# One decoder layer on one core: small weights first, the input projection in two transfers, sums and last roundings of the feed-forward weights on ScalarE

## What is computed

```python
def weight_quant(w):
    wf = w.astype(jnp.float32)
    s = 1.0 / jnp.clip(jnp.mean(jnp.abs(wf)), EPS, None)
    return (jnp.clip(jnp.round(wf * s), -1.0, 1.0) / s).astype(w.dtype)
...
x = x + _L0_attn_ref(_layernorm(x, axis=-1), L0_attn_W_in, L0_attn_conv_w, L0_attn_conv_b, L0_attn_dt_bias, L0_attn_A_log, L0_attn_D_param, L0_attn_norm_w, L0_attn_W_out)
x = x + _L0_xattn_ref(_layernorm(x, axis=-1), ctx_2048, mask_1xSxS2_ff0, L0_xattn_Wq, L0_xattn_bq, L0_xattn_Wk, L0_xattn_bk, L0_xattn_Wv, L0_xattn_bv, L0_xattn_Wo, L0_xattn_qn_w, L0_xattn_kn_w)
x = x + _L0_ffn_ref(_layernorm(x, axis=-1), L0_ffn_w_gate, L0_ffn_w_up, L0_ffn_w_down, L0_ffn_ln_weight)
```

## Time and profile before

| | us |
|---|---|
| median of 3 runs | 1346.29 (1344.91 to 1346.92) |
| the profiled execution | 1347.58 |
| its span, first to last instruction | 1345.7 |
| TensorE matmuls busy | 1241.6 (92%) |
| VectorE busy | 1048.4 (78%) |
| ScalarE busy | 709.5 (53%) |
| GpSimd busy | 767.3 (57%) |

### The profile page before, as it was taken

One profiled execution on the slowest core, in us unless ns is written; L12 is line 12 of the kernel. 1 busy time (PEld: TensorE's weight loads), 2 busy tenths in 40 slices (PEclk: granted clock), 3 DMA queues, 4 the chain that ended last, 5 costly groups with the idle time before them and its releaser, 6 DMA issues.

```text
span 1345.7 us, 31978 instructions
## 1 busy us (share of the span) xinstructions
PE 1241.6 (92%) x10775; PEld 1027.5 (76%) x10807; DVE 1048.4 (78%) x2581; ACT 709.5 (53%) x1611; POOL 767.3 (57%) x1338
## 2 busy tenths in 40 slices
PE   2679999999999999999999999999999999999964
PEld 2568787887777788877878887777788778778743
DVE  3765888887888888888888887888888788888655
ACT  1345555545556555555655555565554556555432
POOL 2344655665565566556556665565566556556541
PEclk9689999999999999999999999999999999999987
DMA  6500000000000000000000000000000000000000
GB/s 193 165 5 6 9 13 13 13 12 12 4 8 12 12 12 12 12 4 8 12 12 12 12 12 8 4 12 12 12 12 12 8 4 12 12 12 9 5 5 9
DMA packets 25761, 24.37 MB, mean 18 GB/s; under 512 B 7168, under 2 KB 24064, under 8 KB 25472
## 3 DMA queue, kind: packets, MB, share of 16 engines
q1 hardware_dynamic: 23376, 20.79, 5.1%
...
## 4 chain that ended last, share of the span: by engine, by line
PE 81%; DVE 10%; issue 3%; POOL 2%; ACT 2%; DMA 1%; SPq 0%; DVEq 0%; POOLq 0%; ACTq 0%
PE bank L1244 17%; PE bank L1334 16%; PE bank L1304 5%; PE bank L1168 4%; PE bank L1177 4%; PE bank L1217 4%; PE bank L1140 3%; PE bank L1157 2%; PE bank L1359 2%; PE bank L1257 2%; PE bank L1314 2%; PE bank L1354 2%; PE bank L1185 2%; PE bank L1372 2%; PE bank L1141 2%
## 5 line engine op out<-in xcount | busy, mean ns | idle before, releaser
L1244 PE MATMUL bank<-xcT,wq 128*128 128x128 f32 x2048 | 237.9, 277 | 2.3 <-ACT xcT L608 2.3
L1244 PEld LDWEIGHTS bank<-xcT,wq 128*128 128x128 f32 x2048 | 232.7, 193 | 7.1 <-issue 2.9
L1334 PE MATMUL bank<-wo,oT 128*128 128x256 f32 x1024 | 233.1, 381 | 0.0
L1334 PEld LDWEIGHTS bank<-wo,oT 128*128 128x128 f32 x1024 | 191.1, 191 | 24.0
L814 DVE SCALAR_TENSOR_TENSOR xc<-bank,cw,xc 128x124 f32<-128x124 f32 (+2 forms) x576 | 163.7, 340 | 7.7 <-ACT xc L570 1.3
L623 ACT ACTIVATE qT<-bank,bqT 128x128 f32<-128x128 f32 x384 | 109.2, 367 | 39.1 <-PE bank L1244 39.1
L389 POOL TENSOR_SCALAR ssy<-ssy 128x1 f32<-128x1 f32 x32 | 6.1, 192 | 197.8 <-DVE ssy L873 197.8
L965 DVE SCALAR_TENSOR_TENSOR h<-h,bank 128x512 f32<-128x512 f32 x64 | 44.0, 688 | 75.5 <-ACT h L662 75.5
L407 POOL TENSOR_TENSOR rq<-rq,minus_half 128x16 f32<-128x16 f32 x32 | 93.3, 2916 | 7.8 <-DVE rq L912 7.8
L429 POOL TENSOR_TENSOR pr<-pr,mx 128x512 f32<-128x512 f32 x64 | 65.6, 1046 | 47.8 <-DVE mx L931 47.8
L419 POOL TENSOR_TENSOR pr<-pr,mask 128x512 f32<-128x512 f32 x64 | 80.1, 1272 | 1.6 <-DVE pr L919 1.6
...
## 6 DMA issues: line engine op xcount, KB each, us to landing
x_in<-in_x SPq DMA_DIRECT2D x32, 128.0 KB, 2.0
c_in<-in_ctx SPq DMA_DIRECT2D x32, 128.0 KB, 2.0
out<-x SPq DMA_DIRECT2D x32, 128.0 KB, 1.7
...
wo<-in_L_xattn_Wo SPq DMA_DIRECT2D x1, 2048.0 KB, 12.6
w_in<-in_L_attn_W_in SPq DMA_DIRECT2D x1, 1288.0 KB, 8.6
...
```

Of the source, the lines that this page charges most:

```text
L1244: last = mm(x_Qbank[g][:, (n % 4) * P:(n % 4 + 1) * P], wq[:, c, n * HD:(n + 1) * HD], xcT[:, c, :], start=(c == 0), stop=(c == DC - 1))
L1334: last = mm(X1[:, 0:D], oT[:, n, :, :], wo[:, n, :], start=(n == 0), stop=(n == NH - 1))
```

## The change

- Loads: the four small weights are issued by ScalarE, first on its queue; SyncE loads `W_in` in two transfers, columns 1024 to 1287 first (`w_bc_l`), the rest after (`w_in_l`). ScalarE issues the three feed-forward matrices only when `w_in_l` has landed. `w_up` lands in `oT`, `w_down` in a new buffer `w_dn`.
- TensorE waits for `w_bc_l` ahead of `m_project_bc` and for `w_in_l` ahead of `m_project_z`, not for the whole matrix at the start.
- GpSimd halves `conv_w` and `conv_b` and negates `a_neg` after the first norm's root, not ahead of it, and scales `w_out` within pass 0.
- The three sums are ScalarE's (Abs with an accumulator, in passes -1, 0 and 0), one `w_total` serves all three, and `w_means` makes the three scales. `w_round` is two VectorE passes; the last rounding, a subtraction with a cast to bf16, is ScalarE's `w_ternary`. `w_gate` is rounded in pass 0, `w_up` in pass 1, `w_down` in pass 2; `w_turn(2)` stands inside pass 2.
- In pass 0 the output product and the residual of tile 0 come ahead of the B/C projection, and the statistics and norm of its attention input are made there too; pass 1 transposes it first of all.

The buffers, and the loads on SyncE:

```diff
+        w_dn = sb("w_dn", [P, 2 * FF])
+        round_c = sb("round_c", [P, 1])
+        w_stage = [qT[:].rearrange("p a h s -> p (a h s)"), oT[:].rearrange("p h a s -> p (h a s)"), w_dn[:]]
+        w_abs = q2[:].rearrange("p a h s -> p (a h s)")
...
-            sp.dma_start(w_in[:], W_in.rearrange("(c p) n -> p c n", p=P)).then_inc(s["w_in_l"].sem, 16)
-            sp.dma_start(cw[:], conv_w.rearrange("(j p) w -> p j w", p=P)).then_inc(s["w_conv"].sem, 16)
-            sp.dma_start(a_neg[:], row(A_log, NHM)).then_inc(s["w_conv"].sem, 16)
-            sp.dma_start(dtb[:], row(dt_bias, NHM)).then_inc(s["w_conv"].sem, 16)
-            sp.dma_start(cb[:], conv_b.rearrange("(j p) -> p j", p=P), allow_slow_non_contiguous=True).then_inc(s["w_conv"].sem, 16)
+            w_cols = W_in.rearrange("(c p) n -> p c n", p=P)
+            sp.dma_start(w_in[:, :, 2 * DI:], w_cols[:, :, 2 * DI:]).then_inc(s["w_bc_l"].sem, 16)
+            sp.dma_start(w_in[:, :, 0:2 * DI], w_cols[:, :, 0:2 * DI]).then_inc(s["w_in_l"].sem, 16)
```

On ScalarE the loads and the new functions:

```diff
+            act.dma_start(cw[:], conv_w.rearrange("(j p) w -> p j w", p=P)).then_inc(s["w_conv"].sem, 16)
+            act.dma_start(dtb[:], row(dt_bias, NHM)).then_inc(s["w_conv"].sem, 16)
+            act.dma_start(a_neg[:], row(A_log, NHM)).then_inc(s["w_conv"].sem, 16)
+            act.dma_start(cb[:], conv_b.rearrange("(j p) -> p j", p=P), allow_slow_non_contiguous=True).then_inc(s["w_conv"].sem, 16)
+            act.wait_ge(s["w_in_l"].sem, 16)
             for n, (w, cols) in enumerate(((w_gate, D), (w_up, D), (w_down, FF))):
                 act.dma_start(w_stage[n].rearrange("p (j n) -> p j n", n=cols), w.rearrange("(j p) n -> p j n", p=P)
                               ).then_inc((s["w_gate_l"], s["w_up_l"], s["w_down_l"])[n].sem, 16)
...
+            def w_sum(n):
+                act.wait_ge((s["w_gate_l"], s["w_up_l"], s["w_down_l"])[n].sem, 16)
+                count(act, s["q_sum"], n)
+                sc.activation(w_abs, w_stage[n], ACT.Abs, accum_out=wsum[:, n:n + 1]).then_inc(s["q_sum"].sem, 1)
+
+            def w_ternary(n):
+                act.wait_ge(s["q_step"].sem, 2 * n + 2)
+                sc.activation(w_tern[n], w_stage[n], ACT.Identity, bias=round_c[:, 0:1]).then_inc(s["q_bf"].sem, 1)
```

On VectorE the means and the rounding, and a piece of the body:

```diff
+            def w_means():
...
+                v.tensor_scalar(wmean[:], F0[:, 0:3], 1.0 / (D * FF), QUANT_EPS, ALU.mult, ALU.max).then_inc(s["q_mean"].sem, 1)
+                dve.wait_ge(s["q_mean"].sem, 1)
+                v.reciprocal(winv[:], wmean[:]).then_inc(s["q_mean"].sem, 1)
+                dve.wait_ge(s["q_mean"].sem, 2)
...
+                v.tensor_scalar(w_stage[n], w_stage[n], winv[:, n:n + 1], ROUND, ALU.mult, ALU.add).then_inc(s["q_step"].sem, 1)
+                dve.wait_ge(s["q_step"].sem, 2 * n + 1)
+                v.tensor_scalar(w_stage[n], w_stage[n], ROUND - 1.0, ROUND + 1.0, ALU.max, ALU.min).then_inc(s["q_step"].sem, 1)
...
-                v.tensor_scalar(w_stage[n], w_stage[n], -1.0, ROUND, ALU.max, ALU.add).then_inc(s["q_step"].sem, 1)
-                dve.wait_ge(s["q_step"].sem, 4 * n + 4)
-                if n == 2:
-                    dve.wait_ge(s["q_t"].sem, 2)
-                v.tensor_scalar(w_tern[n], w_stage[n], ROUND, None, ALU.subtract).then_inc(s["q_bf"].sem, 1)
```

```diff
+                if first == 0:
+                    m_residual(m)
+                    x_stats(m)
```

In GpSimd's body:

```diff
+                if first == -1:
+                    pool.wait_ge(s["w_conv"].sem, 16 * W_CONV)
+                    g.tensor_scalar(cw[:], cw[:], 0.5, None, ALU.mult).then_inc(s["p_scaled"].sem, 1)
+                    g.tensor_scalar(cb[:], cb[:], 0.5, None, ALU.mult).then_inc(s["p_scaled"].sem, 1)
+                    pool.wait_ge(s["p_exp"].sem, 1)
+                    g.tensor_scalar(a_neg[:], a_neg[:], -1.0, None, ALU.mult).then_inc(s["p_scaled"].sem, 1)
+                if first == 0:
+                    pool.wait_ge(s["w_out_l"].sem, 16)
+                    pool.wait_ge(s["w_skip"].sem, 16 * W_SKIP)
+                    g.tensor_tensor(w_out[:], w_out[:], bcast(nw[:, :].unsqueeze(2), [P, XCH, D]),
+                                    ALU.mult).then_inc(s["p_wout"].sem, 1)
```

In TensorE's body:

```diff
+                if first == 1:
+                    x_transpose(xa)
...
+                if first == 0:
+                    pe.wait_ge(s["p_wout"].sem, 1)
+                    m_output(m, xa)
...
+                if first == 2:
+                    w_turn(2)
```

More of the change, by code:

```diff
@@ L458, in body @@
             def body(mn, m, xa, xb, f, fb, first=None):
-                if xa is not None:
+                if xa is not None and first != 1:
                     x_norm(xa)
@@ L707, in body @@
                     m_xnT_copy(mn)
+                if first == 0:
+                    w_sum(2)
                 if xa is not None:
                     x_q_square(xa, 3)
+                if first == 1:
+                    w_turned(0)
+                    w_ternary(1)
                 if xb is not None:
@@ L720, in body @@
                     x_sums_copy(xa, m)
+                if first == 0:
+                    w_ternary(0)
                 if xa is not None:
                     x_k_square(xa)
+                if first == 2:
+                    w_ternary(2)
                 if f is not None:
@@ L732, in body @@
                     m_tanh_z(mn)
+                if first == -1:
+                    w_sum(0)
+                if first == 2:
+                    w_turned(2)
                 if f is not None:
@@ L742, in _ @@
             act.wait_ge(s["p_scaled"].sem, 3)
-            body(*tiles(-1))
-            body(*tiles(0))
+            act.wait_ge(s["c_round"].sem, 1)
+            body(*tiles(-1), first=-1)
+            body(*tiles(0), first=0)
             act.wait_ge(s["w_kv"].sem, 32)
@@ L748, in _ @@
             sc.copy(wv_hi[:], wv).then_inc(s["p_hi"].sem, 1)
-            w_turned(0)
-            act.wait_ge(s["q_bf"].sem, 2)
             act.wait_ge(s["w_small"].sem, 16 * W_SMALL)
             act.wait_ge(s["p_qk"].sem, 2)
-            body(*tiles(1))
+            body(*tiles(1), first=1)
             w_turned(1)
-            w_turned(2)
             act.wait_ge(s["p_lo"].sem, 2)
-            act.wait_ge(s["q_bf"].sem, 3)
-            for i in range(2, 5):
+            body(*tiles(2), first=2)
+            for i in range(3, 5):
                 body(*tiles(i))
@@ L1096, in body @@
                     m_conv_bc(mn)
+                if first == 0:
+                    x_norm(m)
                 if mn is not None:
@@ L1106, in body @@
                     f_stats(xb)
-                if m is not None:
+                if m is not None and first != 0:
                     m_residual(m)
@@ L1448, in body @@
                     x_sums_turn(xa, m)
+                if first == -1:
+                    pe.wait_ge(s["w_bc_l"].sem, 16)
+                if first == 0:
+                    pe.wait_ge(s["p_wout"].sem, 1)
+                    m_output(m, xa)
                 if mn is not None:
@@ L1453, in body @@
                 if first == -1:
-                    w_total(0)
-                if first == 0:
-                    pe.wait_ge(s["p_wout"].sem, 1)
-                if m is not None:
+                    pe.wait_ge(s["w_in_l"].sem, 16)
+                if m is not None and first != 0:
                     m_output(m, xa)
@@ L1477, in _ @@
             w_turn(1)
-            w_turn(2)
             pe.wait_ge(s["w_attn"].sem, 16 * W_ATTN)
+            body(*tiles(2), first=2)
             pe.wait_ge(s["q_evac"].sem, 6)
-            for i in range(2, 5):
+            for i in range(3, 5):
                 body(*tiles(i))
```

79 lines of the change are left out of this document (26 added, 53 removed).

## The result

The changed kernel takes 1344.22 us in the median of 20 runs (1340.20 to 1346.40), the kernel before 1346.99 in as many (1344.76 to 1348.34). The ratio is 0.9981, interval 0.9973 to 0.9988: 2.8 us faster, a quarter of the 11.6 that were forecast. That is at the 0.2% which the prediction put between faster and no change, and 1344.22 lies outside its range of 1329.5 to 1340.5.

A forecast was written before the change was run, and what follows sets the result against it. TensorE's stream of passes was taken as the bound, so only its earlier start counts. Terms -7.2 - 1.4 - 0.9 - 3.9 + 0.4 + 1.4 = -11.6 took 1346.3 to 1334.7 us, range 1329.5 to 1340.5.

The forecast's parts named there:

- The start: Loads up to the first copy of the normalised tile: copy at 13.25 in place of 20.47, -7.2 us.
- Alone at the head of ScalarE's queue, from 2.0 on, the same rate puts them in at 9.5: Start: the four small loads, 1,792 short runs at 240 a us, land at 9.5 in place of 17.35.
- I take 9.5 + 1.8 = 11.3 for the moment when ScalarE is free: Start: after the small loads the queue drains 500 to 700 feed-forward rows, so ScalarE's issues end at 11.3.
- held longer: Rival at the start: small runs drain slower or the third issue lasts 4.74 after them; -4.3, 1337.6 us, chance 0.18.
- its sign of being wrong: Start: the forecast counts as wrong if the first copy comes outside 10 to 16 us.
- Pass 0: Pass 0 and its seam to pass 1: queries at 60.4, before 61.83, on the old scale; -1.4 us.
- The attention input is copied by 60.4: Seam to pass 1: ScalarE copies `x` at about 59.4, then the attention input by 60.4, letting the queries start.
- Pass 1: Pass 1, queries to sums: shorter queries and no 1.38 us wait for the square; -0.9 us more than pass 0.
- The seam: Behind pass 1, between key copy and scores: the second transposes and all copies leave the 4.05 us; -3.9 us.
- What is given back: Behind the seam: GpSimd's three constants and the logarithm stand ahead of VectorE's earlier next norm; +0.4 us.
- Pass 2: Pass 2 takes over the `w_down` passes (+0.3) and transposes (+1.1); +1.4 us.
- the sum puts it at nothing, since ScalarE has the cover: Three last roundings moved to ScalarE, about 1.9 each against 1.23 on VectorE, cost nothing; the skill's rule says 2.0 us.

The follow-up runs named there:

- key constant early: Changed kernel with GpSimd's two products for the key weight `qk_w` moved into pass 0: 1341.52 us, ratio 0.9958 to the kernel before.
- skip loads last: Changed kernel with SyncE's loads of `D_param` and `norm_w` moved behind `w_out` and `c_in`: 1342.88 us, ratio 0.9968 to the kernel before.
- three edits: Changed kernel with `qk_w` made in pass 0, `D_param` and `norm_w` loaded behind `c_in`, then feed-forward loads on SyncE: 1336.80 us, ratio 0.9924 to before.

## Why the prediction was wrong

**The start: -7.2 forecast, -2.5 measured.** Two steps failed, both sizes. The first is "Alone at the head of ScalarE's queue, from 2.0 on, the same rate puts them in at 9.5". It was not alone among short runs: `D_param` and `norm_w` come next on SyncE's queue, and the small loads were in at 14.2. Without those two they are in at 10.8, still 1.3 late: 204 runs a microsecond from 2.0 on, not 240. The second is "I take 9.5 + 1.8 = 11.3 for the moment when ScalarE is free". The reading behind it held: the trace's DMA records count about 1,470 runs issued and not started on ScalarE's queue when the third issue returned before, and about 1,840 after (about 1,820 with the key constant early, 1,770 with the skip loads last). But there was nothing to drain at speed: the runs of `w_gate` stand behind those of `conv_b`. ScalarE was free at 16.1, later than the 14.2 that I gave as the bound of "held longer". That rival was right in kind, and its price too small. With both repaired the first copy comes at 11.53, and at 10.55 with `conv_b` first; the forecast was 13.25, its early bound 10.2. The changed kernel's 17.99 lies outside the 10 to 16 that the prediction gave as its sign of being wrong.

On the rule that the prediction takes from the Trainium skill, DMA: Bandwidth & Descriptors, "Issuing engines are not separate DMA queues": by it a move between queues saves only issue time. The trace agrees, if issue time is taken as it was here. With the feed-forward loads on SyncE `conv_b` lands at 14.2 as before that edit, and what is saved is 3.0 us of the first copy, since ScalarE's compute stands behind its issues.

**Pass 0: -1.4 forecast, +1.8 measured.** "The attention input is copied by 60.4" left out one wait of ScalarE ahead of its copy of `x`, that for GpSimd's `qk_w`. It cost nothing before, since TensorE's work ended later. I had costed GpSimd's `w_out` product, not what stands at the end of GpSimd's preparations, nor that VectorE's passes would slow it: the rounding of `w_up` at the start of pass 1 is counted as nothing, though the trace of before had GpSimd steps of 1.28 and 1.18 beside such passes. Without the wait the term is -1.8 in one trace and the step holds. With all three edits it is 52.41 - 11.53 - 41.36 = -0.5, with 3.4 us more at the low clock.

**Pass 1: -0.9 forecast.** From the queries to the sums 81.09 - 61.83 = 19.26 before; 16.79 and 17.87 in the two traces after, 18.01 with the three edits. That is -1.2 with the wait repaired and up to -2.5 without. Part of the work of pass 1 had been done during the wait there, and in this stretch the kernel before ran 6.8 us at the low clock (62.2 to 65.6 and 75.9 to 79.3), the first trace of after and the three edits 3.4. So -0.9 is right in size as far as the clock lets one see.

**The seam: -3.9 forecast,** 5.0 by the two traces (the clock was low from 82.7 to 86.1 before, not after), 3.96 by the experiment that undoes it: right. What is given back was under-sized: 1.05 where +0.4 was forecast. **Pass 2: +1.4 forecast,** 36.88 to 38.20 measured: right.

**The third rounding on ScalarE.** The step "the sum puts it at nothing, since ScalarE has the cover" held; the rule for adds and multiplies of the Trainium skill (ScalarE: Activation LUTs, "Rules for kernel authors") would have made the moves cost 2.0 us. The runs do not agree: undoing them gains nothing, and costs 0.8 to 2.8 with the wait out of the way. In these passes the engine with room counts, not the unit price, which was 1.23 on VectorE against 2.06 on ScalarE (the `w_ternary` of pass 1).

**The sum.** In the kernel with three edits the queries of pass 3 are 13.3 us earlier than before (124.61 against 137.89): the start -8.9, pass 0 -0.5, pass 1 and the seam -6.2, and 1.1 and 1.3 given back. The forecast was 11.6, and the change as made got 5.7 by its first trace, 4.0 by the second. In the first, 4.7 of the shortfall are the start and 3.2 pass 0; pass 1 and the seam gave 2.6 more than forecast, which the clock can account for: the kernel before ran 6.8 us more of this stretch at half speed, worth up to 3.4. So 11.6 is not far from what the two repairs reach, in part by luck: the start came out earlier than forecast, pass 0 later. What is left open is the tail: with the three edits the last 65.7 us ran at 0.74 in place of 0.79 and took back 2.5 us. What decides it was not tried. One and the same kernel has mean clocks of 0.977 and of 0.982 from run to run, but all 5 runs with the three edits were at 0.977 or 0.978, where with the last rounding on VectorE added 5 of 6 were at 0.980 or more, and its trace had the short end.
